# Four steps of VectorE and one ternary product change places in the tail of a quantized attention kernel

## The reference

```python
q = x + embed[stage][..., None]            # bias per row
prob = softmax(q @ f.T, axis=-1)
xh = (prob @ f) @ H                        # H: Hadamard matrix / 16
scale = max(max(abs(xh), axis=-1), 1e-5) / 7
xq = clip(round(xh / scale), -8, 7) * scale
out = x + xq @ ternary(weight).T           # ternary: -1, 0, 1 times a row scale
```

## Time and profile before

| | us |
|---|---|
| median of 3 runs | 102.9 |
| lowest and highest run | 101.88, 104.1 |
| the profiled execution | 102.76 |
| its span in the trace | 100.9 |
| busy PE, PEld, DVE, ACT, POOL | 90.6, 83.9, 79.1, 71.3, 70.9 |

### The profile page before, as it was taken

How to read it: one execution, slowest core, us unless ns; L and a number is a source line. 1 busy time by engine, 2 the same in 40 slices (tenths; PEclk the granted TensorE clock), 3 DMA queues, 4 the chain that set the end, 5 groups by cost and what they waited for, 6 DMA issues and landing times.

```text
span 100.9 us, 2542 instructions
## 1 busy us (share of the span) xinstructions
PE 90.6 (90%) x734; PEld 83.9 (83%) x734; DVE 79.1 (78%) x197; ACT 71.3 (71%) x185; POOL 70.9 (70%) x107
## 2 busy tenths in 40 slices
PE   5999898948599989999999999999999999999640
PEld 2379887948499979999999999999999999989410
DVE  1338597998549796988989797979796979798881
ACT  3558768775748796959596959695969595776820
POOL 4152270999778596959697979897889886505870
PEclk9999999999999999999999999999999999999999
DMA  2919804202758947464738473938283222321125
GB/s 74 300 71 317 300 6 113 101 0 104 161 154 263 107 119 226 134 206 133 226 98 265 113 251 82 282 93 270 63 292 82 86 53 103 66 97 44 60 107 205
DMA packets 14591, 14.71 MB, mean 146 GB/s; under 512 B 7922, under 2 KB 8568, under 8 KB 14584
## 3 DMA queue, kind: packets, MB, share of 16 engines
q1 hardware_dynamic: 14272, 14.36, 48.5%
q10 hardware_dynamic: 312, 0.27, 0.8%
HBM read 8.72 MB, written 4.19 MB: 128 GB/s over the span
## 4 chain that ended last, share of the span: by engine, by line
PE 68%; DVE 10%; DMA 7%; POOL 6%; issue 3%; ACT 3%; DVEq 0%; POOLq 0%
PE xh_bank L492 19%; PE score_bank L492 14%; PE fh_bank L492 12%; DMA code_t<-code 7%; PE out_bank L546 6%; PE q_bank L481 5%; PE prob_bank L481 5%; PE out_bank L461 4%; POOL code L371 2%; ACT q_hi L677 2%; POOL f_lo L331 1%; DVE q_lo L886 1%; POOL w_over_above L396 1%; DVE xh_bank L1028 1%; ACT code L681 1%
## 5 line engine op out<-in xcount | busy, mean ns | idle before, releaser
L703 ACT ACTIVATE prob<-score_bank,neg_max 128x256 f32<-128x256 f32 x30 | 13.9, 470 | 13.7 <-DVE neg_max L910 13.7
L379 POOL TENSOR_TENSOR result<-scaled,x_all 128x512 f32<-128x512 f32 x12 | 15.4, 1286 | 10.5 <-DVE scaled L872 10.5
L331 POOL TENSOR_TENSOR f_lo<-ft,f_hi 128x512 fp32r<-128x512 f32 x13 | 17.0, 1310 | 0.0
L845 DVE TENSOR_REDUCE abs_max<-xh_bank 128x2 f32<-128x512 f32 x14 | 9.7, 691 | 8.7 <-PE xh_bank L492 8.7
L492 PE MATMUL fh_bank<-had,f_hi 128*128 128x256 f32 x64 | 14.0, 300 | 0.0
L371 POOL TENSOR_TENSOR code<-code,magic 128x512 bf16<-128x512 f32 x13 | 13.5, 1041 | 0.5 <-ACT code L681 0.3
L681 ACT ACTIVATE code<-xh_bank,inv_scale 128x256 f32<-128x256 f32 x30 | 13.0, 498 | 0.4 <-DVE inv_scale L869 0.3
L492 PE MATMUL score_bank<-f_hi,q_hi 128*128 128x256 f32 x60 | 13.2, 301 | 0.0
L492 PE MATMUL fh_bank<-had,f_lo 128*128 128x256 f32 x64 | 12.7, 280 | 0.0
L872 DVE SCALAR_TENSOR_TENSOR scaled<-out_bank,out_scale,w_scale_row 128x256 f32<-128x256 f32 x27 | 11.8, 476 | 1.0 <-PE out_bank L546 1.0
L492 PE MATMUL xh_bank<-fh_hi,prob_hi 128*128 128x256 f32 x60 | 12.1, 283 | 0.1
(11 more groups left out here) (142 smaller groups left out, 228.2 us busy)
## 6 DMA issues: line engine op xcount, KB each, us to landing
ft<-f_turned_dram SPq DMA_DIRECT2D x16, 256.0 KB, 2.7
x_all<-x_dram SPq DMA_DIRECT2D x16, 256.0 KB, 2.8
out_dram<-result SPq DMA_DIRECT2D x14, 256.0 KB, 2.0
w_t<-weight_turned_dram SPq DMA_DIRECT2D x1, 256.0 KB, 3.0
out_dram<-result SPq DMA_DIRECT2D x2, 128.0 KB, 1.8
out_dram<-last_result ACTq DMA_DIRECT2D x2, 128.0 KB, 1.8
code_t<-code SPq DMA_TRANSPOSE x13, 2.5
had_block<-hadamard_dram SPq DMA_DIRECT2D x1, 64.0 KB, 2.9
```

The costliest lines, as they stand in the source:

```text
L331: nc.gpsimd.tensor_tensor(f_lo[:, b.k], ft[:, b.k], f_hi[:, b.k].bitcast(F32), ALU.subtract).then_inc(f_lo_ready, 1)
L379: nc.gpsimd.tensor_tensor(result[:, b.k], as_rows(scaled[:, b.k]), x_all[:, b.at], ALU.add).then_inc(result_ready, 1)
L703: a = nc.scalar.activation(prob[:, t], score_bank[:, t], ACT.Exp, bias=neg_max[:, b.k, t:t + 1], accum_out=row_sum[:, b.k, t:t + 1])
L845: nc.vector.tensor_reduce(abs_max[:, :], xh_bank[:, :, :], AX.X, ALU.max, apply_absolute_value=True).then_inc(abs_max_ready, 1)
```

## The change

On TensorE, `turn_prob(last)` goes ahead of `turn_code(third_last)`, and the ternary product of the third-last batch goes from ahead of the last batch's mix to between its two tiles. The wait for `prob_ready` ahead of it goes (turn_prob has it). On VectorE, the output scales of the third-last batch are taken out of `scales`, and the two maxima of the last batch go ahead of them and of fh's low part; behind the maxima come fh_lo(14), prob_lo(14), the output scales of 13, the inverse sums of 14, the output of 12, then a wait for the output scales of 13 (their operand inv_sum has the same buffer as that of 15), and the rest as before. No instruction that computes is added or removed, and ScalarE, GpSimd and SyncE keep their programs.

```diff
@@ TensorE
             times_ternary(fourth_last)
             times_hadamard(last)
+            turn_prob(last)
             turn_code(third_last)
-            turn_prob(last)
             mix(second_last)
-            pe.wait_ge(prob_ready, B)
-            pe.wait_ge(code_t_ready, third_last.at + 1 - turned_by_dma)
-            for t in range(T):
-                mm = ternary_tile(third_last_out_bank, t, third_last)
-            mm.then_inc(third_last_out_in_bank, 1)
             pe.wait_ge(prob_hi_ready, B)
             pe.wait_ge(fh_lo_ready, B)
             for t in range(T):
                 product(last_xh_banks[t], mixed(last), [t],
                         wait_for_last_part=lambda: pe.wait_ge(prob_lo_ready, B)
                         ).then_inc(last_xh_in_bank, 1)
+                if t == 0:
+                    pe.wait_ge(code_t_ready, third_last.at + 1 - turned_by_dma)
+                    for u in range(T):
+                        mm = ternary_tile(third_last_out_bank, u, third_last)
+                    mm.then_inc(third_last_out_in_bank, 1)
@@ VectorE
-            def scales(b, out_on_pool=True):
+            def scales(b):
 ...
                 wait(dve, abs_max_ready, b.at + 1)
-                if out_on_pool:
-                    wait(dve, least_ready, b.at + 1)
-                    row_inverse(b)
-                else:
-                    row_scales(b, out_scale[:, b.k])
-
-            def row_scales(b, to_out):
                 wait(dve, least_ready, b.at + 1)
                 row_inverse(b)
+
+            def row_scales(b, to_out):
                 for t in range(T):
 ...
-            scales(third_last, out_on_pool=False)
-            split_fh(second_last)
-            inverse_sums(second_last)
+            scales(third_last)
             for t in range(T):
                 dve.wait_ge(score_in_bank, last.at + t + 1)
                 nc.vector.tensor_reduce(neg_max[:, last.k, t:t + 1], last_score_banks[t][:, t],
                                         AX.X, ALU.max,
                                         negate=True).then_inc(neg_max_ready, 1)
+            split_fh(second_last)
             split_prob(second_last)
+            row_scales(third_last, out_scale[:, third_last.k])
+            inverse_sums(second_last)
             scale_out(fourth_last)
+            dve.wait_ge(out_scale_ready, third_last.at + 1)
             inverse_sums(last)
             split_fh(last)
             split_prob(last)
```

## The result

The changed kernel takes 104.23 us (median of 20 runs, 102.83 to 105.8) against 103.78 us for the kernel before (median of 20 runs, 101.88 to 104.59). The ratio, taken between undisturbed runs, is 1.0096, 95% interval 1.0055 to 1.0137: slower by about 1 us. The forecast was +0.62 us, 103.5.

What follows compares the result with a forecast made beforehand. TensorE is busiest, but from 92.33 VectorE's chain sets the end. First half's +0.16 is covered by ScalarE's +0.73 less 0.11 slack: +0.62 in all, 102.9 + 0.6 = 103.5 us, range 102.4 to 104.5.

Steps and rivals of the forecast that it cites:

- Maxima: VectorE, batch 15: maxima go first, second starts at 88.50 instead of 89.03, idle about 0.35, probabilities ready 0.43 earlier.
- Who takes it?: TensorE's turn of prob takes the 0.43 gain, but 0.37 is lost waiting for prob's low part of batch 14.
- TensorE stands idle from 89.90 to 90.16: TensorE ahead of the turn of prob: idle until prob's low part of batch 14 ends, codes now being turned behind.
- The turns: TensorE: batch 13's codes turned behind prob, so the mix of batch 14 starts at 90.80, 0.16 later.
- VectorE covers itself: VectorE ahead of batch 14's maximum: free at 92.38, 0.11 before the mix result at 92.49, so its added work costs nothing.
- The ternary product: Batch 13's product on TensorE 0.88 later; through ScalarE's queue quantizing of batch 14 0.73 later, VectorE's decode 0.62 later.
- the slack of 0.11: Time from batch 14's turned codes on TensorE to VectorE's decode at 95.17, less 0.04 for release: 0.11 us spare.
- The lead: Rival: earlier maxima bring the mix 0.10 forward and the late ternary product costs ScalarE nothing; 102.8, chance 8%.
- the clock: Rival: TensorE's clock drops to 1.2 GHz after longer idle ahead of batch 14's codes, +0.8 more, 104.3; chance 5%.
- GpSimd's last output scale: Ends at 97.31, 0.26 before VectorE wants it; rival: GpSimd later than counted holds VectorE's final outputs, 104.0, chance 10%.
- first half: The maxima and turns part: +0.16 on VectorE's chain, covered by the delay on ScalarE's route.
- no measurement of this kernel tells such a change from nothing: Remark on the forecast of 103.5 us, 0.6% slower: too small for a measurement of this kernel to distinguish.

Runs made afterwards that it cites:

- Run 1: The changed kernel with the fh product of batch 15 sent to score_bank, so without the wait for fh's low part; ratio to the kernel before 1.0056.
- run 2: The changed kernel with fh's low part of batch 14 back ahead of the two maxima; ratio to the kernel before 0.9996.
- run 7: Kernel before, TensorE unchanged; VectorE: fh's low part (14), maxima, prob's low part, then output scales (13), inverse sums (14); ratio 1.0049.

## Why the prediction was right in part: direction and ternary product right, the wait for fh_bank missed

- **Maxima (right).** Second maximum forecast at 1.87 behind the anchor, measured 1.86; VectorE's idle is 0.28 (forecast 0.35). The exponentials end at 91.16 - 88.11 = 3.05 (forecast 3.12).
- **"Who takes it?" (the step that failed).** I named one waiter for the gain, the turn of prob, and of its two waits the low part of prob. The maxima went past fh's low part, and I asked only who waits for the maxima. Who waits for the low part itself I did not ask, beyond the mix. TensorE's fh product of batch 15, which stands ahead of that turn in the same queue, waits for it, to overwrite fh_bank. "TensorE stands idle from 89.90 to 90.16" was wrong: TensorE stood idle ahead of the fh product, and then no more. Run 1 prices this: 0.39. In the terms of the sum, the mix was forecast 0.16 late and was 0.67 late (run 1: 0.28). With the measured value the forecast's own sum comes out: 0.67 and 0.72 for the tile make the scaling 1.39 late, less 0.21 in ScalarE's queue and 0.11 of slack is 1.07, against 1.09 at the end.
- **The trace before did show it,** in rows that the prediction did not use:

```profile
88.30 0.61 PE L546 MATMUL out_bank<-tern_t,code_t 128*128 128x256 bf16 x4
88.84 0.30 PEld L492 LDWEIGHTS fh_bank<-had,f_hi 128*128 128x128 f32 x2 [0.22 <-issue]
88.87 0.48 PE L492 MATMUL fh_bank<-had,f_hi 128*128 128x256 f32 x2
```

The fh product started 0.57 behind the ternary product of 12, which takes only 0.36 to the next start where nothing waits (87.60 to 87.96 in run 1). The low part ended at 88.04 + 0.68 = 88.72. So this wait already held the fh product, by 0.2 us, and every step put ahead of the low part makes that product later by as much. The view names the idle only "issue".
- **The turns (right in kind).** +0.28 alone, where the forecast had the mix 0.16 late with the maxima moved too, and the run's expectation was 0.2. In the change it cost 0.05, since the fh product had taken the idle away.
- **VectorE covers itself (right, narrowly).** Batch 14's maximum was released by TensorE in the changed kernel, after an idle of 0.23. Since the mix was later than forecast, run 1 is the closer test: the idle was 0.17 there.
- **The ternary product (right).** Alone 0.41, through ScalarE's queue, with the slack of 0.11 as read. In the change the scaling was 1.39 late for 0.88 forecast; the surplus of 0.51 is the mix's, which was 0.67 late for 0.16.
- **Rivals.** The lead did not arrive; the clock did not fall, and where TensorE idled for 0.96 ahead of the codes of batch 14 (forecast 1.03) the granted clock stayed at 1.00, that is 2.4 GHz. The Trainium skill's rule ("TensorE: Matmul & The Clock Gate", part 1) would have brought it down after an idle that is long enough; no run here shows that at work in the tail. GpSimd's last output scale began at 99.14 and ended at 99.34, 0.18 ahead of its reader at 99.52: a spare of 0.18 for 0.26 forecast, so it did not decide.

```profile
96.20:97.60 1.40, 0.44 (x6) 0.23 (x4) 1.08 (x6) 1.40 (x5) 1.02 (x1) 1.00 0.00 0
```

(The window of the changed kernel around TensorE's idle: length, each engine's busy us, then the granted clock, 1.00, against the earlier trace rows.)

The sum as it came out: wait for fh_bank 0.39, other moves of the first half and the ternary product 0.70 together (forecast 0.62), in all 1.09 in the traces and 1.0096 as a ratio, that is about 1.0 us. The 0.08 that run 1 has over the forecast comes from the mix, 0.12 later than forecast (0.28 for 0.16), less 0.06 that ScalarE's queue absorbed more than counted; the rest is 0.02 behind the decode. Most of the 0.12 is the turn's start, 0.15 behind its releaser's end (89.41 to 89.56) where I had counted 0.04; this was not tested by itself.

The time alone does not refute +0.62 us: that is a ratio of 1.006, inside the interval of 1.0055 to 1.0137. The traces do, and so the failed step stands on them. But the prediction's remark that no measurement of this kernel tells such a change from nothing did not hold: the interval of the 20 runs leaves out 1.

## What to carry to other kernels

When an instruction is moved past another, list the waiters of the one that is passed over, not only of the one that is moved; above all the engine that wants to overwrite what it still reads. A product that starts a few tenths later behind its predecessor than elsewhere, with no releaser named, may stand at a wait: look in the code which one. And a queue that is served in order turns a late cheap step (a scaling for a batch that is not urgent) into a late urgent one behind it; what it takes away is the lateness less the slack in front of each of the two.

## What was not expected of the hardware

The executions of one kernel spread over 2.7 us here (101.88 to 104.59 for the kernel before), and the traces show where most of it lies: ahead of the first maximum over xh_bank, which started at 15.66 us in the profiled execution before, at 17.69 in the changed one, at 15.20 in run 2 and 17.63 in run 7, with the same instructions in the same order. In the late ones TensorE's early matmuls take longer. In the kernel before and in the changed one, at the first scores:

```profile
8.03 0.40 PE L492 MATMUL score_bank<-f_lo,q_hi 128*128 128x256 f32 x2
8.26 0.40 PE L492 MATMUL score_bank<-f_hi,q_lo 128*128 128x256 f32 x2
```

```profile
9.13 0.63 PE L492 MATMUL score_bank<-f_hi,q_hi 128*128 128x256 f32 x2
9.55 0.63 PE L492 MATMUL score_bank<-f_lo,q_hi 128*128 128x256 f32 x2
...
10.75 0.41 PE L492 MATMUL score_bank<-f_lo,q_hi 128*128 128x256 f32 x2
```

Two matmuls start every 0.42 us in place of every 0.24, until about 10.4 us. The granted clock stands at 1.00 in the windows of both kernels there, so that record does not show the slower pace; the starts do. Why some executions have it stays open. A change in the tail that is worth under 1 us is better judged against an anchor in the trace than by the span.

How soon TensorE resumed behind a wait depended on what it waited for. Behind VectorE's low parts it took 0.15 us: from the end of fh's low part (90.99) to the first matmul (91.14) in the changed kernel, from prob's low part in run 1 (89.41 to 89.56), and from fh's low part in the kernel before (88.72 to 88.87). Behind ScalarE's codes it took 0.05 (96.39 + 0.84 to 97.28), behind VectorE's decode 0.06 (97.72 + 0.42 to 98.20). VectorE and ScalarE resumed 0.04 behind TensorE (94.06 + 0.40 to 94.50, 95.01 + 0.61 to 95.66), though the ends of matmuls in these views are modelled. Why the low parts differ was not tested.
